# Natural order of the rows between the two stages, block order written by the first normalisation of the second

## The reference, cut to what matters

```
x = x + tanh(g_xattn) * mixer(ctx, ctx, layernorm(x), ssm_kernel, D, 8)
x = x + tanh(g_ffn)   * ffn(layernorm(x), ln_w, ln_b, W1, b1, W2, b2)

mixer(k, v, q, taps, D):      # per head of 8 rows, L = 1024
    kv  = outer products of the rows of k and v
    out = causal convolution of kv with taps, + kv * D
    return sum over i of out[i, j] * q[i]

ffn(inputs, ...):
    x = bf16(inputs); residual = x
    h = bf16(layernorm(x) * ln_w + ln_b)
    h = bf16(mx_quant(h) @ mx_quant(W1).T + b1)
    h = bf16(gelu(h))
    h = bf16(mx_quant(h) @ mx_quant(W2).T + b2)
    return bf16(residual + h)
```

## Time and profile before

| what | us |
|---|---|
| median of three runs | 2108.7 |
| lowest, highest | 2106.93, 2108.92 |
| the profiled execution's own time | 2109.22 |
| its span, first to last instruction | 2107.4 |
| PE busy | 1936.4 (92%) |
| DVE busy | 1713.9 (81%) |
| ACT busy | 736.8 (35%) |
| POOL busy | 915.4 (43%) |

### The profile page before, as it was taken

One profiled execution on the slowest core, in us unless ns is written; L12 is line 12 of the kernel. 1 busy time (PEld: TensorE's weight loads), 2 busy tenths in 40 slices (PEclk: granted clock), 3 DMA queues, 4 the chain that ended last, 5 costly groups with the idle time before them and its releaser, 6 DMA issues.

```text
span 2107.4 us, 29465 instructions
## 1 busy us (share of the span) xinstructions
PE 1936.4 (92%) x11776; PEld 1493.9 (71%) x11776; DVE 1713.9 (81%) x2091; ACT 736.8 (35%) x1028; POOL 915.4 (43%) x1036
## 2 busy tenths in 40 slices
PE   6999999999999999999232579999999999999998
PEld 5888888888888888888231456666666666666663
DVE  6888788888888878887799888888888898888844
ACT  3222222222222222222141444444444444545440
POOL 4888888888888888888501000000000000000000
PEclk9999999999999999999655789999999999999999
DMA  5445445444544544542568201111111111111111
GB/s 196 147 163 183 151 156 176 163 143 170 172 149 155 182 159 153 171 153 98 188 213 280 78 21 61 61 61 45 55 53 60 61 61 41 51 61 61 41 41 70
DMA packets 61160, 247.62 MB, mean 117 GB/s; under 512 B 7200, under 2 KB 7200, under 8 KB 52832
## 3 DMA queue, kind: packets, MB, share of 16 engines
q1 hardware_dynamic: 61024, 245.74, 34.0%
HBM read 211.57 MB, written 34.14 MB: 117 GB/s over the span
## 4 chain that ended last, share of the span: by engine, by line
PE 43%; DVE 7%; issue 1%; DMA 0%; ACT 0%; POOL 0%; DVEq 0%; POOLq 0%; ACTq 0%
PE acc_ps L670 21%; PE l_ps L655 21%; DVE arena L915 2%; DVE f_o_res L915 2%; DVE w_T L930 1%; DVE arena L930 1%; PE tr_ps L633 1%; DMA arena<-in_w 0%; DVE f_stats L782 0%; DVE f_stats L781 0%; DVE arena L881 0%; DVE arena L891 0%; DVE f_amax_x L826 0%; DVE f_o_res L920 0%; DVE arena L920 0%
## 5 line engine op out<-in xcount | busy, mean ns | idle before, releaser
L217 PE MATMUL y_ps<-kk_hi,slab 128*128 128x512 f32 (+8 forms) x3072 | 870.6, 366 | 5.3 <-DMA slab<-taps_scratch 5.3
L217 PEld LDWEIGHTS y_ps<-kk_hi,slab 128*128 128x128 f32 x3072 | 557.7, 188 | 101.5 <-DMA slab<-taps_scratch 5.7
L217 PE MATMUL y_ps<-kk_lo,slab 128*128 128x512 f32 (+8 forms) x1536 | 561.9, 366 | 0.0
L655 PE MATMUL l_ps<-f_xq_T,w_T 128*128 128x256 bf16 x4096 | 457.7, 275 | 68.4 <-ACT arena L735 66.1
L655 PEld LDWEIGHTS l_ps<-f_xq_T,w_T 128*128 128x128 bf16 x4096 | 403.6, 99 | 123.2 <-ACT arena L735 66.7
L670 PE MATMUL acc_ps<-w_T,arena 128*128 128x512 bf16 x2048 | 449.0, 379 | 0.0
L670 PEld LDWEIGHTS acc_ps<-w_T,arena 128*128 128x128 bf16 x2048 | 198.8, 98 | 232.2
L991 POOL TENSOR_TENSOR f_rstd<-f_var_eps,f_neg_half 128x1 f32<-128x1 f32 x32 | 21.8, 682 | 741.9 <-DVE f_var_eps L794 741.9
L217 PEld LDWEIGHTS y_ps<-kk_lo,slab 128*128 128x128 f32 x1536 | 289.8, 189 | 47.5
L735 ACT ACTIVATE arena<-l_ps,f_b 128x256 bf16<-128x256 f32 x512 | 213.7, 471 | 279.8 <-PE l_ps L655 221.9
L453 POOL TENSOR_TENSOR lsum<-lower 128x240 f32<-128x240 f32 (+1 forms) x128 | 254.8, 1991 | 122.8 <-DVE lower L359 122.8
(11 more groups left out here) (101 smaller groups left out, 1954.1 us busy)
## 6 DMA issues: line engine op xcount, KB each, us to landing
slab<-taps_scratch SPq DMA_DIRECT2D x128, 512.0 KB, 4.4
arena<-in_w_m SPq DMA_DIRECT2D x32, 1024.0 KB, 6.9
arena<-x_scratch SPq DMA_DIRECT2D x64, 512.0 KB, 3.9
arena<-in_w SPq DMA_DIRECT2D x32, 1024.0 KB, 4.9
k_ext<-in_ctx_e SPq DMA_DIRECT2D x64, 384.0 KB, 3.0
x_tile<-in_x_t SPq DMA_DIRECT2D x32, 512.0 KB, 4.7
x_scratch<-x SPq DMA_DIRECT2D x32, 512.0 KB, 2.9
out_t<-arena SPq DMA_DIRECT2D x32, 512.0 KB, 2.6
```

Source lines behind the costliest of these rows:

```text
L217: mm = nc.tensor.matmul(y_ps[:, y_base + begin:y_base + end], slab[s][:, half, d * P:(d + 1) * P], kk_part[s][:, begin - d * PAIR:end - d ...
L655: mm = nc.tensor.matmul(l1_ps[bank % L1_BANKS][:, a, :], w1_T[:, k, col:col + P], xq_T[:, k, :], start=(k == 0), stop=(k == L // P - 1))
```

## The change

`residual` now writes natural order: one addition of 1024 contiguous elements in place of two strided ones of 512. `first_norm` reads natural order and writes `n_bf` in block order (the order in which DVE weighs and quantises it, as before): the same instruction, with its output elements 32 bf16 elements (64 bytes) apart. On the host, the columns of W2, `b2` and the output keep natural order; `ln_w` and `ln_b` stay in block order. `norm_again` and the final addition have the lines that they had, on data in natural order.

```
             def residual(t):
                 ...
-                out = x1[t % 2][:].rearrange("p (i k) -> p k i", k=L // QB)
-                x = x_tile[:, t % X_SLOTS, :].rearrange("p (k i) -> p k i", i=QB)
-                back = turn_ps[:].rearrange("p n (k i) -> p (n k) i", i=QB)
-                half = L // QB // 2
-                nc.vector.tensor_tensor(out[:, 0:half, :], back[:, 0:half, :], x[:, 0:half, :], ALU.add)
-                nc.vector.tensor_tensor(out[:, half:, :], back[:, half:, :], x[:, half:, :], ALU.add).then_inc(x1_ready, 1)
+                nc.vector.tensor_tensor(x1[t % 2][:], turn_ps[:].rearrange("p n c -> p (n c)"), x_tile[:, t % X_SLOTS, :],
+                                        ALU.add).then_inc(x1_ready, 1)
             ...
             def first_norm(t):
                 ...
-                nc.scalar.activation(n_bf[t % GROUP][:], xin[t % X_LOADS], ACT.Identity, bias=shift1[:, col:col + 1],
-                                     scale=rs[:, col:col + 1]).then_inc(n_ready, 1)
+                nc.scalar.activation(n_bf[t % GROUP][:].rearrange("p (i k) -> p k i", k=nb1),
+                                     xin[t % X_LOADS].rearrange("p (k i) -> p k i", k=nb1), ACT.Identity,
+                                     bias=shift1[:, col:col + 1], scale=rs[:, col:col + 1]).then_inc(n_ready, 1)
...
-    w2 = by_blocks(np.asarray(L0_ffn_W2), 0, L)
+    w2 = np.asarray(L0_ffn_W2)
...
-        "b2": by_blocks(np.asarray(L0_ffn_b2), 0, L),
+        "b2": L0_ffn_b2,
...
-    got = got.reshape(tiles, TILE_HEADS, HD, B, QB, L // QB).transpose(3, 0, 1, 2, 5, 4)
+    got = got.reshape(tiles, TILE_HEADS, HD, B, L).transpose(3, 0, 1, 2, 4)
```

## The result

The changed kernel took 2113.5 us in the median of nine runs (2111.91 to 2114.46); the kernel before, nine runs beside them, 2107.56 us (2105.7 to 2109.48). The ratio is 1.0028, with a 95% interval of 1.0017 to 1.0038: slower by 3.6 to 8 us, 5.9 us in the medians. The forecast was 2109.7 us, 1.0 us over the kernel before, and no difference that a measurement could tell. The measured time stands on the last value of the range, and it got there by rival 3.

A forecast was written before the change was run, and what follows sets the result against it. PE was taken to bound stage one and the feed-forward groups. A gain of 0.66 us at stage one's end and a loss of 1.67 us behind group 0 summed to + 1.0 us: 2109.7 us, range 2106.0 to 2113.5.

The forecast's parts named there:

- rival 3: ACT's strided normalisation far slower than DVE's rows say, holding PE: 2114.3 us at 4.6 us each, up to 2140; chance 0.07.
- L714 over 3.9 us: Sign of being wrong: the first normalisation's rows on ACT, expected at about 2.3 us, read over 3.9 us.
- The addition: Stage one, DVE: 2.15 us becomes 1.22 us a tile, worth nothing for 31 tiles, 0.66 us gained at the last.
- The strided write: First normalisation on ACT, writing bf16 64 bytes apart: 2.3 us where contiguous took 1.24; 1.67 us lost behind group 0.
- The bound that I had set for the two-byte element: Upper end for the normalisation's strided bf16 write on ACT: a doubling once more, 4.6 us, kernel 2114.3 us.
- 2D - 2.93: Loss where PE resumes behind group 0 after two normalisations, for D over 1.69 us; 1.67 us at D = 2.3.
- D: Time of one first normalisation on ACT with the strided write, taken as 2.3 us.
- thresholds for later groups: No loss there at D = 2.3; DVE's cover holds until D = 3.3, ACT's until 5.0, PE stops from 6.8.
- Rival 1: ACT's strided write is free, 1.24 us, and PE's restart behind group 0 doesn't move: 2108.0 us; chance 0.15.
- rival 4: The additions pace stage one in a way PE's records hide: faster by at most 30 us, 2079; chance 0.04.
- rival 5: The one contiguous addition is no cheaper than before, leaving + 1.67 alone: 2110.4 us; chance 0.03.
- Rival 2: TensorE's clock comes back later at the restart behind group 0, costing 1.9 us more: 2111.6 us; chance 0.12.

The follow-up runs named there:

- e1: The kernel before with only the residual addition made one contiguous instruction of 1024 elements, first normalisation still contiguous: 2106.61 us against 2108.1, ratio 0.9994.
- e8: The changed kernel with the strided write in 30 of 32 normalisations; tiles 4 and 5 read strided, write contiguously: 2108.34 us against the kernel before's 2107.87, ratio 1.0002.
- e3: The changed kernel with the first normalisation reading floats 128 bytes apart and writing bf16 contiguously: 2108.56 us against the kernel before's 2108.1, ratio 1.0002.
- e2: The kernel before with only the first normalisation's write strided, bf16 64 bytes apart: 2113.68 us, ratio 1.0027.
- e5: The changed kernel with the normalisations of tiles 4 and 5 moved behind bank 6 of group 1: 2107.72 us against the kernel before's 2107.87, ratio 0.9998.
- e4: The changed kernel plus a block of 1024-element copies, 17 forms on ACT, 9 on DVE: ACT bf16 written 64 bytes apart 4.83 us, DVE 2.39.
- e9: The changed kernel plus a second block of copies, eight forms on ACT, three on DVE: ACT's aligned bf16 pairs 1.24 us, moved pairs 3.13.

## Why the prediction was right, and where not

**The number: inside the range by luck.** I forecast a difference of + 1.0 us; measured were + 5.9. On the base that I counted from, 2108.7 us, the same difference would have given 2114.6, outside the range. The kernel before read 2107.56 us beside the changed one, and that 1.1 us alone puts the time on 2113.5, the range's last value. By my own figures this was the case with a chance of 0.07, slower by more than the 4.2 us that I called the least one can tell; and one of my signs of being wrong, L714 over 3.9 us, was met.

**What bounds the kernel: right.** PE sets the time of stage one and of the later groups; e1 shows the first, e8 the second. Two sentences read the list of waits too broadly. There is a wait of PE for DVE in it,

```profile
PE acc_ps L643 <- DVE arena L930: 63.5, 16, 15.5
```

but line 643 turns weights, behind stage one; and the "twice in the whole kernel" that PE waits for ACT holds for layer 1's wait for the bias additions (655 for 735), not for every wait. Neither touches the argument.

**The addition: right.** 1.22 us for the new form by L899's row; 1.224 us measured. Zero for 31 tiles, 0.66 us for the last: both as read in the profile.

**The strided write: wrong, and this is the step that failed.** "The edit on ACT is a write, as L400's is, so I go by that row": 2.3 us; measured 4.95 us in the mean. L400 writes floats, the edit writes bf16. The forms show how much that is: at any distance from 16 bytes on ACT needs 2.1 to 2.2 us for floats, nearly what I took, and 4.7 to 4.9 us for bf16. DVE has the same trait, 1.03 against 2.39 us. The bound that I had set for the two-byte element, 4.6 us, was close (2114.3 for the kernel, measured 2113.5), but I gave rival 3, to which it belongs, a chance of 0.07 on the ground that "no strided row costs over 2 times"; there was no row of a strided two-byte write at all, on any engine, so that ground carried nothing. Nor does a factor carry over: on a plain DVE copy floats 128 bytes apart cost 1.03 against 0.69 us, 1.5 times, where L400, an addition out of PSUM, had 1.88.

**Where it lies on the path: right.** The law 2D - 2.93 at the restart gives 6.97 us for D = 4.95. Measured were 6.24 at PE, because the second of a pair starts while the first still writes: from 1224.54 to 1233.81 the two take 9.27 us, not 9.9. With 2D replaced by 9.27 the law gives 6.34. The thresholds for later groups held too. At D = 3.3 DVE's idle time ends: DVE now waits 28 times, 55.7 us, and in e3, with D = 2.18, twice, 1.6 us. At D = 5.0 ACT's cover ends: with a pair of 9.44 us ACT's wait for PE ahead of its first bias addition is 0.61 us where it was 7.12, and PE wasn't touched:

```profile
1448.96 9.44 ACT L710 ACTIVATE f_n<-arena,f_shift,f_rstd 128x1024 bf16<-128x1024 f32 x2 [4.50 <-POOL f_shift L990]
1459.02 0.84 ACT L732 ACTIVATE arena<-l_ps,f_b 128x256 bf16<-128x256 f32 x2 [0.61 <-PE l_ps L651]
```

The last threshold, 6.8, was not tried.

**The rivals.** Rival 3 is what happened, by its first stage only. Rival 1 (a free write) falls by 4.95 us, rival 4 by e1, rival 5 by 1.224 us. Rival 2, a clock that comes back later, did not show: the 208 products behind the restart took 0.26 us more, at a mean granted clock of 0.92 after and 0.93 before, and in other profiles they took 25.44 us behind a stop of 11.80 (e8) but 25.00 behind one of 16.45 (e2). So a longer stop does not by itself make them longer, and 0.26 us between two single profiles is no effect that can be told.

The Trainium skill ("Advanced Engine Details and Errata", Memory Cachelines), by which an access to another 16-byte line each time pays, gave the sign. The section names no engine; the forms show the penalty on ACT and on DVE, with different sizes. They agree that nothing gets dearer beyond 16 bytes. They differ on two accesses a line, which by that section absorb the latency: floats 8 bytes apart are nearly free (1.30 us), bf16 8 bytes apart are not (2.66 us). Here the measurement decides.

## What to carry to other kernels

Price a strided operand by a row with the same engine, the same side (read or write) and the same element size, and where there is none, let the range hold the worst and give it a real chance. When a bf16 row must change its order on the way through ACT or DVE, stride the read and keep the write contiguous, or write at least whole four-byte words. For floats the side made no difference on ACT: 2.1 us for either. An instruction that grows fourfold in 32 places may cost at one place only: look for the place where its engine is the one that PE waits for, and ask first whether it must stand there in the queue. And a cover that was read while PE was late is smaller once PE is not (e5).

## What the runs showed of the hardware that I had not expected

ACT copies 1024 elements in 1.24 us when it reads and writes contiguously. With a strided write (e4), single bf16 take 1.52 us at 4 bytes distance, 2.66 at 8, and 4.7 to 4.9 from 16 to 128 bytes; single floats take 1.30 at 8 bytes and 2.1 to 2.2 from 16 to 128. Pairs of bf16 64 bytes apart take no more than a contiguous write (1.24 us) if they are aligned to four bytes, and 3.13 us if they are not (e9). Reads with a stride and a contiguous write take 2.1 us, for floats 128 bytes apart as for bf16 64 bytes apart (e4). DVE copies in 0.69 us contiguously, and in 2.39 us with single bf16 written 64 bytes apart (e4).
